# Longer key and value transfers, mask rows inside the score contraction, a transposition that sums, and zero products in an audio tower

## The reference, cut to what matters

```python
# x [64, 4000]
frames = x[:, idx]                        # 64 x 25 frames of 100 samples, step 160
h = log(mel(|rfft(frames * window)|**2) + 1e-6) @ dct.T @ w_proj + b_proj      # [64, 25, 192]
# Hyena convolution, order 2
z  = shortconv3(layernorm(h) @ W_lin.T + b_lin)       # three streams of 192 channels
v  = z2 + layernorm(h)
for i in range(2):
    v = v + softmax(z_i over the channels) * fftconv(h_i, v)
h = h + v + v @ W_out.T + b_out
# causal attention, 12 heads of 16 channels over T = 25 frames
q, k, v = split(layer_norm(layernorm(h), ln1_w) @ c_attn_w.T)
s   = where(causal, q @ k.T / 4, -inf)
an  = layernorm(h) + (softmax(s) @ v) @ c_proj_w.T
# 8 experts, each token goes to its best 2; an expert takes 400 tokens, in token order
h = h + an + sum over e of p(e) * gelu(layer_norm(an) @ c_fc[e]) @ c_proj_e[e]
```

## Time and profile before

| | |
|---|---|
| median of 3 runs | 424.59 us (422.98 to 426.7) |
| the profiled execution | 425.44 us, of which the span is 423.6 us |
| token phase with a steady rhythm (SP's keys of tile 0 to tile 15) | 68.93 to 255.09 us |
| first expert's first product | 298.70 us |
| PE busy | 340.2 us (80%) |
| DVE, ACT, Pool busy | 220.3, 184.3, 182.5 us |
| data moved | 26.96 MB, mean 64 GB/s |

### The profile page before, as it was taken

How to read it: one execution, slowest core, us unless ns; L and a number is a source line. 1 busy time by engine, 2 the same in 40 slices (tenths; PEclk the granted TensorE clock), 3 DMA queues, 4 the chain that set the end, 5 groups by cost and what they waited for, 6 DMA issues and landing times. The chain is left out here.

```text
span 423.6 us, 8602 instructions
## 1 busy us (share of the span) xinstructions
PE 340.2 (80%) x2851; PEld 259.6 (61%) x2851; DVE 220.3 (52%) x689; ACT 184.3 (44%) x528; POOL 182.5 (43%) x325
## 2 busy tenths in 40 slices
PE   3886687889998997998998796420799999999990
PEld 2332245556665664766666474320699999999980
DVE  1114423446674776475677633332557766676430
ACT  1240243354654455354455432130657656685330
POOL 5011011112335564266455544755025756686644
PEclk9999999897997999797999958655599999999995
DMA  7600600414212222112111111200744544410002
GB/s 203 202 24 0 238 2 9 124 31 99 68 31 49 46 51 37 36 40 35 31 31 32 31 26 31 37 15 9 208 129 112 141 74 131 113 32 1 8 2 29
DMA packets 53170, 26.96 MB, mean 64 GB/s; under 512 B 40559, under 2 KB 49814, under 8 KB 53000
## 3 DMA queue, kind: packets, MB, share of 16 engines
q1 hardware_dynamic: 44728, 20.13, 20.2%
q10 hardware_dynamic: 1232, 4.87, 3.3%
q0 software_dynamic: 7168, 1.43, 2.7%
HBM read 17.42 MB, written 10.98 MB: 67 GB/s over the span
## 5 line engine op out<-in xcount | busy, mean ns | idle before, releaser
L1390 POOL DMA_INDIRECT out<-ye,tok x32 | 66.9, 2092 | 57.6 <-DVE ye L1264 51.5
L745 PE MATMUL psum<-wprh,hidh 128*100 128x192 f32 x192 | 49.0, 255 | 0.3 <-DVE hidl L1255 0.3
L746 PE MATMUL psum<-wprl,hidh 128*100 128x192 f32 x192 | 48.4, 252 | 0.0
L747 PE MATMUL psum<-wprh,hidl 128*100 128x192 f32 x192 | 48.4, 252 | 0.0
L1362 POOL DMA_INDIRECT slots<-xl,atu x32 | 34.2, 1068 | 8.7 <-issue 7.5
L730 PE MATMUL psum<-xeTh,wfch 96*128 96x400 f32 x96 | 34.3, 357 | 0.8 <-DVE xeTl L1228 0.8
L1255 DVE TENSOR_TENSOR hidl<-gelu,hidh 128x400 fp32r<-128x400 f32 x48 | 27.0, 572 | 13.0 <-ACT gelu L978 12.5
L731 PE MATMUL psum<-xeTl,wfch 96*128 96x400 f32 x96 | 33.7, 352 | 0.0
L1044 DVE TENSOR_TENSOR prod<-psum,hcoef 73x768 f32<-73x768 f32 x32 | 30.4, 952 | 6.2 <-PE psum L521 6.1
L732 PE MATMUL psum<-xeTh,wfcl 96*128 96x400 f32 x96 | 33.5, 349 | 0.0
L745 PEld LDWEIGHTS psum<-wprh,hidh 128*100 128x100 f32 x192 | 31.7, 165 | 0.4 <-DVE hidl L1255 0.4
(11 more groups left out here) (208 smaller groups left out, 850.4 us busy)
## 6 DMA issues: line engine op xcount, KB each, us to landing
wfc<-in_c_fc SPq DMA_DIRECT2D x6, 576.0 KB, 5.0
wpr<-in_c_proj_e SPq DMA_DIRECT2D x6, 576.0 KB, 5.8
slots<-fill ACTq DMA_DIRECT2D x5, 490.0 KB, 4.5
xe<-slots SPq DMA_DIRECT2D x8, 306.2 KB
kx<-qk SPq DMA_DIRECT2D x96, 12.5 KB, 1.9
vdram<-v SPq DMA_DIRECT2D x16, 96.0 KB
pack_ffn<-in_ffn SPq DMA_DIRECT2D x1, 1332.5 KB, 13.6
vx<-vdram SPq DMA_DIRECT2D x64, 18.8 KB
```

Source lines behind the costliest of these rows:

```text
L745: mm(dst, hidh[:, m, qs], wprh[:, e % 2, m], start=m == 0, stop=False)
L746: mm(dst, hidh[:, m, qs], wprl[:, e % 2, m], start=False, stop=False)
L747: last = mm(dst, hidl[:, m, qs], wprh[:, e % 2, m], start=False, stop=m == MC - 1)
L1390: pool.indirect_dma_start(out, bass.IndirectOffsetOnAxis(ap=tok[e % 2][:, q:q + 1], axis=0), ye[e % 2][:, q], None, bounds_check=TOKENS - ...
```

## The change

1. **Keys.** `kx` is laid out [rows, 6 heads, half, 100]: each of the six transfers now has 16 rows of one run of 200 numbers (800 B).
2. **Values.** The value columns of the projection's weight are reordered on the host, so that each of the four transfers has 25 rows of 4 runs of 48 numbers (192 B). yT's stationary operand takes every third number of `vx`.
3. **Mask.** `qk` and `kx` get 25 more rows, filled once at the start by four new loads (`in_qmask` 25x400, `in_kmask` 25x1200, each twice, 320 KB), so that the 8 score products contract 121 rows and bring the mask with them. `identb`, `causalb` and their casts go, and so do 300 columns of the weight load `in_ffn`. The four loads stand in SP's queue ahead of the second load of frames.
4. **Zero products in s.** Ahead of its waits for keys and queries, s issues 2 bf16 products of zeros, 300 columns each.
5. **vT.** Pool's vb goes. PE issues 3 bf16 products of zeros and then four f32 products with the identity, two for v1 and, after a wait for g1, two for g1, which add up in PSUM.
6. **Pool's order.** After idx now come ef, base, scatter, pn and last meta (the tags that go with a token's row).
7. **Zero products at two waits.** Ahead of the wait for the last tile's `chosen`, pos issues 12 products of zeros of 512 columns; ahead of e_xT(0) there are 34.

```diff
             load(pack["hyena"][:], a["hyena"], "in_hyena")
+            for p in range(2):
+                load(qk[p][DC:].rearrange("p n c t -> p (n c t)"), a["qmask"], "in_mask")
+                load(kx[p][DC:].rearrange("p h c t -> p (h c t)"), a["kmask"], "in_mask")
             load(frames[:, 2 * R:], a["frames"][:, 2 * R:], "in_frames")
...
                 for h in range(HQ):
-                    sp.dma_start(kx[i % 2][h * HD:(h + 1) * HD, :, :, h * T:(h + 1) * T],
-                                 qk[i % 2][h * HD:(h + 1) * HD, 1].rearrange("p c (b t) -> p c b t", t=T))\
+                    sp.dma_start(kx[i % 2][h * HD:(h + 1) * HD, h],
+                                 qk[i % 2][h * HD:(h + 1) * HD, 1])\
                         .then_inc(S[f"kxd{i % 2}"], 16)
...
-                src = vdram[i % 3].rearrange("p b (g h d) -> h p b g d", g=NG, h=HG)
                 for h in range(HG):
-                    sp.dma_start(vx[i % 2][h * T:(h + 1) * T].rearrange("p b (g h d) -> p b g h d", g=NG, h=HG)[:, :, :, h],
-                                 src[h, 0:T]).then_inc(S[f"vxd{i % 2}"], 16)
+                    hd = slice(h * NG * HD, (h + 1) * NG * HD)
+                    sp.dma_start(vx[i % 2][h * T:(h + 1) * T, :, h], vdram[i % 3, 0:T, :, hd])\
+                        .then_inc(S[f"vxd{i % 2}"], 16)
...
+            def zeros(dst, n):
+
+                for _ in range(n):
+                    mm(dst, zero[:, 0:W], zero[:, 0:dst.shape[-1]], start=True, stop=True)
...
             def vT(i):
-                pe.wait_ge(S["v2"], i + 1)
+                pe.wait_ge(S["v1"], i + 1)
...
-                tr(pvTa, v2[i % 2][:, 0:DA], ident[:])
-                tr(pvTb, v2[i % 2][:, DA:], ident[:]).then_inc(S["vT"], 1)
+                zeros(pvTa, 3)
+                mm(pvTa, v1[i % 2][:, 0:DA], ident[:], start=True, stop=False)
+                mm(pvTb, v1[i % 2][:, DA:], ident[:], start=True, stop=False)
+                pe.wait_ge(S["g1"], i + 1)
+                mm(pvTa, g1[i % 2][:, 0:DA], ident[:], start=False, stop=True)
+                mm(pvTb, g1[i % 2][:, DA:], ident[:], start=False, stop=True).then_inc(S["vT"], 1)
...
-                pe.wait_ge(S["qks"], i + 1)
-                landed(pe, "kxd", 2, i, HQ)
+                    pe.wait_ge(S["in_mask"], 16 * 4)
+                need(pe, "h1", min(i + 2, NT))
                 need(pe, "xp", min(i + 2, NT))
                 need(pe, "an", min(i + 2, NT))
                 need(pe, "sc", i)
-                mm(ps, identb[:], causalb[:], start=True, stop=False)
+                zeros(ps, 2)
+                pe.wait_ge(S["qks"], i + 1)
+                landed(pe, "kxd", 2, i, HQ)
                 for c in range(2):
                     for b in range(G):
-                        last = mm(ps[b * STRIP:b * STRIP + T, c * HQ * T:(c + 1) * HQ * T],
-                                  qk[i % 2][:, 0, c, b * T:(b + 1) * T], kx[i % 2][:, c, b], start=False, stop=c == 1)
+                        last = mm(strips(ps[b * STRIP:(b + 1) * STRIP, c * HQ * T:(c + 1) * HQ * T]),
+                                  qk[i % 2].rearrange("p n c t -> p (n c t)")[:, c * R + b * T:c * R + b * T + STRIP],
+                                  kx[i % 2][:, :, c, b * T:(b + 1) * T], start=True, stop=True)
...
-                    return mm(pyT[half * GD:(half + 1) * GD, col * T:(col + 1) * T], vx[i % 2][:, b, g * GD:(g + 1) * GD],
+                    return mm(pyT[half * GD:(half + 1) * GD, col * T:(col + 1) * T], vx[i % 2][:, b].rearrange("p h (d g) -> p g (h d)", g=NG)[:, g],
                               pT[i % 2][:, g, b * T:(b + 1) * T], start=True, stop=True)
...
             def pos(i):
+                if i == NT - 1:
+                    pe.wait_ge(S["g0"], NT)
+                    pe.wait_ge(S["prod1"], NT)
+                    zeros(PB[1], 12)
                 pe.wait_ge(S["chosen"], i + 1)
...
+            pe.wait_ge(S["prod1"], NT)
+            zeros(PB[2], 34)
             e_xT(0)
...
-            def vb(i):
-                pool.wait_ge(S["g1"], i + 1)
-                ptt(v2[i % 2], v1[i % 2], g1[i % 2], ALU.add).then_inc(S["v2"], 1)
...
                 run(idx, j - 10)
-                run(meta, j - 9)
+                run(ef_, j - 8)
                 run(base_, j - 8)
-                run(ef_, j - 8)
-                run(vb, j - 4)
                 run(scatter, j - 10)
                 run(pn_, j - 6)
+                run(meta, j - 9)
```

More of the change, by code:

```diff
@@ L75, in constants @@
     c["wc3"] = sel
-    causal = np.zeros((W, HEADS, T))
-    causal[rows] = np.where(t[None, None, :] > np.tile(t, G)[:, None, None], MASKED, 0.0)
-    c["causal"] = causal
+    late = np.zeros((T, 2, 2, G, T))
+    late[:, 0] = np.where(t[:, None] > t[None, :], MASKED, 0.0)[:, None, None]
+    c["qmask"] = late.reshape(T, 4 * R)
+    c["kmask"] = np.tile(np.eye(T)[:, None], (1, HQ * 2 * G, 1)).reshape(T, HQ * 2 * R)
     before = np.zeros((W, W))
@@ L101 @@
     "ffn": (W, [("ln1", W, 2), ("ln2", DC, 2), ("wqa", W, 3 * D + E), ("wqb", W, 3 * D + E),
-                ("wo", W, 2, D + E), ("won", W, 2, 2 * W), ("causal", W, HEADS, T), ("before", W, W), ("ones", W, W),
+                ("wo", W, 2, D + E), ("won", W, 2, 2 * W), ("before", W, W), ("ones", W, W),
                 ("expert", W, E), ("token", W, NT), ("pad", W, 1)]),
@@ L155, in tower @@
         ln1, ln2, wqa, wqb, wo, won = (view[n] for n in ("ln1", "ln2", "wqa", "wqb", "wo", "won"))
-        causal, before, ones, expert = (view[n] for n in ("causal", "before", "ones", "expert"))
+        before, ones, expert = (view[n] for n in ("before", "ones", "expert"))
         token, pad = view["token"], view["pad"]
-        identb = sb("identb", [W, W], BF16)
-        causalb = sb("causalb", [W, HEADS * T], BF16)
         beforeb = sb("beforeb", [W, W], BF16)
@@ L169, in tower @@
         epsc = sb("epsc", [128, 3])
+        zero = sb("zero", [W, 512], BF16)
         fill = sb("fill", [W, FQ, ROW])
@@ L236, in tower @@
         g1 = many(2, "g1", [W, D])
-        v2 = many(2, "v2", [W, D])
         vTA = many(2, "vTA", [W, W])
@@ L249, in tower @@
         aT = many(2, "aT", [W, 2, W])
-        qk = many(2, "qk", [DC, 2, 2, R])
+        qk = many(2, "qk", [DC + T, 2, 2, R])
         v = many(4, "v", [W, D + E])
-        kx = many(2, "kx", [DC, 2, G, HQ * T])
-        vx = many(2, "vx", [HG * T, G, D])
+        kx = many(2, "kx", [DC + T, HQ, 2, R])
+        vx = many(2, "vx", [HG * T, G, HG, NG * HD])
         smax = many(2, "smax", [W, HEADS])
@@ L311, in valid @@
             return x.rearrange("p (b s) -> p b s", s=STRIP)[:, :, 0:T]
-        for name in ("in_tok", "in_frames", "in_lin", "in_taps", "in_hyena", "in_out", "in_ffn", "in_exp0", "in_exp1", "filled",
+        for name in ("in_tok", "in_frames", "in_lin", "in_taps", "in_mask", "in_hyena", "in_out", "in_ffn", "in_exp0", "in_exp1", "filled",
                      "stored0", "stored1", "stored2", "scattered0", "scattered1", "scattered2",
@@ L884, in qks_ @@
                 need(act, "s", i - 1)
-                f(qk[i % 2].rearrange("p n c t -> p n (c t)"), pqk, ACT.Copy).then_inc(S["qks"], 1)
+                f(qk[i % 2][0:DC].rearrange("p n c t -> p n (c t)"), pqk, ACT.Copy).then_inc(S["qks"], 1)
             def v_(i):
@@ L983, in _ @@
             tt, ts, stt = ve.tensor_tensor, ve.tensor_scalar, ve.scalar_tensor_tensor
+            ve.memset(zero[:], 0.0)
             ve.memset(epsc[:, 0:1], EPS)
@@ L1110, in constants_bf @@
                 ve.wait_ge(S["in_ffn"], 16)
-                ve.tensor_copy(causalb[:], causal.rearrange("p h t -> p (h t)"))
                 ve.tensor_copy(beforeb[:], before[:])
-                ve.tensor_copy(onesb[:], ones[:])
-                ve.tensor_copy(identb[:], ident[:]).then_inc(S["prep_ve"], 1)
+                ve.tensor_copy(onesb[:], ones[:]).then_inc(S["prep_ve"], 1)
             def smax_(i):
@@ L1271, in _ @@
             for p in range(2):
-                pool.memset(kx[p], 0.0)
+                pool.memset(kx[p][0:DC], 0.0)
                 pool.memset(vx[p], 0.0)
@@ L1438, in layout @@
     w = d["L0_ffn_c_attn_w"].T
+    vals = w[:, 2 * D:].reshape(D, NG, HG, HD).transpose(0, 2, 3, 1).reshape(D, D)
+    w = np.concatenate([w[:, 0:2 * D], vals], 1)
     w = np.concatenate([w, np.zeros((D, E), w.dtype)], 1)
```

## The result

The changed kernel takes 431.31 us (median of 14 runs, 426.21 to 438.19) beside 424.8 for the kernel before: a ratio of 1.0115 with a 95% interval of 1.0083 to 1.0148, slower by about 1%. The forecast was 411 in a range of 400 to 426; it failed in its direction. The medians of the experiments stand beside those of the kernel before that were taken with them, 425.2 to 425.8; ratios leave disturbed runs out, medians don't, and the changed kernel's own runs spread wide.

A forecast was written before the change was run, and what follows sets the result against it. SP's queue was taken as the bound, PE close behind. Rounds -12.3, first scores -1.0, start +2.5 and +1.2, drain -3.0, warm start -1.2 made -13.8 from 425.44: 411.6 profiled, 411 median, range 400 to 426.

The forecast's parts named there:

- What bounds the kernel: Token phase: SP's queue sets the rhythm, 12.70 us a tile early and 11.75 later, with PE close behind.
- Keys and values: SP's transfer issues: keys 0.602 to 0.50 us, values 0.717 to 0.53, saving 1.36 us a tile.
- That issue time does not follow the runs: Rival on SP's issues: longer runs issue no faster, PE's savings hide under SP, 427 us; chance 0.10.
- the warm start: First expert after the 34 zero products: it runs at full clock, -1.2 us.
- PE's round: PE per tile in the token phase: 11.74 us early, 11.07 later, which decides the steady gain of 12.3 us.
- the rival of the strided weight load: yT on PE: taking every third number doubles weight loads, steady gain is nothing, 424 us; chance 0.10.
- Start-up: Before the first tile: mask loads delay the second frames load, +2.5 us; first vT's added products, +1.2.
- First scores: PE's idle 1.93 us before s(0): six shorter key issues give 1.0 us back.
- Drain: From the last keys to the experts: shorter issues 2.1 us earlier, Pool's order -0.9, together -3.0.
- Zero products: PE's two waits at the token phase's end: 12 take at most 5.5 us; 34 take 11.1, fitting narrowly in 12.1.
- The clock: PE's clock in the rounds: no half-clock stretches, 3.4 us each; rival of five stretches, 424 us, chance 0.07.

The follow-up runs named there:

- the run with the short forms: The changed kernel with keys read from DRAM and values as 25 plain rows of one run, same number of transfers and bytes: 417.68 us, ratio 0.9825.

## Why the prediction was wrong

- **What bounds the kernel** was right: SP's queue, with PE close behind. That 1.56 us less on SP give the kernel before about 10 us confirms it. Not all of SP's round is issues: in the kernel before it waits 29.0 us in 13 rounds from 100 to 262 us for the values that it sent to DRAM to land, some 2.2 a tile, and no run tried to fill that.
- **Keys and values, the step that failed first.** I put keys at 0.50 and values at 0.53, between a plain store and their own rows, as if shorter runs were what made them long. They stayed at 0.589 and 0.717. SP saves 6 x 0.013 = 0.08 us a tile by the medians and not 1.36, and nothing once the key issues of 1 to 1.6 us are counted. That issue time does not follow the runs was a rival, priced at 0.10 and 427; it is the one that held. Its time is 4 short, as the start cost 2.3 more than it has, and the end and the warm start gave 1.7 less. The row of x<-x pointed that way: plain rows, and the longest issue of all.
- **PE's round, the step that failed beside it.** I took 11.07 late; it is 11.91. A product of 128 columns in the transposition takes 0.36 to 0.42 and not 0.22, a length that I had scaled from products of another shape, whose weight loads start ahead of them; with three zero products the transposition is 1.68 and not 1.06. And yT has 0.46 more, the rival of the strided weight load: half of the 1.0 that it was priced at. So even with the transfers as short as forecast there would have been no 12.3 us: in the run with the short forms, which take 2.7 a tile off SP, PE's round is 11.93, above SP's old 11.75. Its profile is 4.9 shorter than the changed kernel's from tile 0 to tile 15 (181.11 against 186.03), and 4.9 in the drain, where fewer issues lie ahead of the last values. The wait of 0.76 that I booked as a gain of the summing transposition goes by Pool's order alone.
- **Start-up**, forecast +2.5 and +1.2, measured +3.7 and +2.3. The 25-row loads hold back the frames for longer than their bytes at the rate of the first slices; PE's wait grew by 4.67 (from 0.52 to 5.19) while the product came 3.66 later, and 4.2 later than with the mask loads behind. By the Trainium skill ("DMA: Bandwidth & Descriptors", why a DMA increments its semaphore by 16) the estimate was about 5. The trace lies between the two, by the 4.2 on that estimate's side. The rule itself was not tested, as no run changed the number of rows.
- **First scores**: PE no longer waits there. It lies inside the rounds, whose sum is unchanged.
- **Drain**, forecast -3.0, measured -0.4: the 2.1 for shorter issues fell with the first step. What Pool's new order gives fits within the 0.4.
- **Zero products**: hidden, as forecast, but the 34 took 9.13 and not 11.1, because about 8 of them passed at half clock where I had counted 15, and the wait was 13.06 and not 12.1. The margin that I feared on the one side was missing on the other; the warm start of -1.2 did not come. Its price was too low too: 2.4 when the gap is filled.
- **The clock** in the rounds did as forecast: 1.00 from 120 to 262, against 0.88 and 0.89 in the same phase before; one stretch at 0.52 was left, from 113.30 to 120.10, where I had taken none. The rounds did not get shorter by it, as work had been added to PE.

## What to carry to other kernels

A queue that issues back to back is shortened by fewer issues or by another queue, and by another form only if a row of that very form shows it; four stores moved to another engine's queue gave here what longer runs did not. Before work is added to the engine that stands second, its round is to be summed from rows of the same shape, and a wait that it has is to be looked at first: here another order on Pool took it away, with no work added to PE. When the bound moves, the second engine's length is the whole gain. Work that only keeps a clock up must reach to the moment at which it is needed.

## What the runs showed of the hardware that was not expected

- Issue time on SP: 25 rows of 4 runs of 192 B from DRAM 0.717 us, of 12 runs of 64 B 0.717, of one run of 768 B 0.298; 16 rows of 800 B from SBUF to SBUF 0.589, from DRAM 0.420; 16 rows of 8 runs from SBUF 0.602.
- A weight load of 64 columns with a step of 12 bytes takes 174 ns (median) against 138 for neighbouring numbers. The Trainium skill ("SBUF — State Buffer", the box on cachelines) asks for two hits in each 16-byte line; the direction agrees, and it gives no size.
- An f32 product of 128 columns in the transposition takes 0.36 to 0.42 us, one of 100 columns in the projection of queries and keys 0.17. By its columns the former would take 0.22. The trace shows where the other 0.15 lies: the weight loads of the second to fourth product start with the product and not ahead of it (L573 211.52 for 211.53, L628 209.00 for 209.09). In the transposition the stationary operands have 128, 64, 128 and 64 columns in turn, in the projection always 96; that this change is the reason was not tried.
- Behind a wait of 3.92 us at the end of the zero products the first expert ran at a granted clock of 0.52, though the clock still read 1.00 in the wait; behind a wait of 0.30 it ran at 1.00.
